# A decoder layer on one core: the order of transfers in SyncE's queue

## The reference

```python
x = layernorm(x + attn(x, w_qkv, b_qkv, w_proj, b_proj))   # causal, 16 heads of 16
x = layernorm(x + slot_attention(x, ctx_1024, ...))        # 3 rounds, GRU cell
x = layernorm(x + mixture_of_experts(x, ...))              # 16 experts, 4 of them kept
# attn
att = einsum('bhqd,bhkd->bhqk', q, k) / sqrt(16); att[not causal] = -inf
y = einsum('bhqk,bhkd->bhqd', softmax(att), v); return y @ w_proj + b_proj
```

## Time and profile before

| what | us |
|---|---|
| median of 3 runs (807.25 to 810.77) | 810.53 |
| the profiled execution | 807.89 |
| its span, first to last instruction | 805.9 |
| attention with its prologue, up to the first context transpose on PE | 239.4 |
| idle time of PE up to 250 us that ended with a DMA of negated maxima | 9.5 |
| idle time of PE up to 250 us that ended with a DMA of operands | 11.8 |

### The profile page before, as it was taken

How to read it: one execution, slowest core, us unless ns; L and a number is a source line. 1 busy time by engine, 2 the same in 40 slices (tenths; PEclk the granted TensorE clock), 3 DMA queues, 4 the chain that set the end, 5 groups by cost and what they waited for, 6 DMA issues and landing times. The chain is left out here.

```text
span 805.9 us, 14338 instructions
## 1 busy us (share of the span) xinstructions
PE 676.9 (84%) x5241; PEld 621.4 (77%) x5256; DVE 478.1 (59%) x1013; ACT 322.1 (40%) x706; POOL 231.3 (29%) x257
## 2 busy tenths in 40 slices
PE   6576989989938899989999799997888657887976
PEld 4454777867727899988989789997888657886976
DVE  3543457647534567676667767676776635546363
ACT  3223435536724345433444344543444224242331
POOL 7112324324421132222230223212243025141432
PEclk9778889989988999989999999999999969989999
DMA  7766255364012000000000000000000000000000
GB/s 239 218 171 202 76 174 155 115 190 105 16 57 101 1 1 1 15 13 0 0 0 26 0 0 0 0 0 1 1 1 2 1 1 1 26 0 26 13 14 27
DMA packets 25676, 40.07 MB, mean 50 GB/s; under 512 B 2336, under 2 KB 11424, under 8 KB 25632
## 3 DMA queue, kind: packets, MB, share of 16 engines
q1 hardware_dynamic: 25632, 39.49, 16.1%
HBM read 24.67 MB, written 14.68 MB: 49 GB/s over the span
## 5 line engine op out<-in xcount | busy, mean ns | idle before, releaser
L1037 DVE TENSOR_REDUCE neg_max<-bank 128x2 f32<-128x512 f32 (+1 forms) x96 | 65.5, 690 | 84.1 <-PE bank L1467 55.2
L1682 PE MATMUL bank<-attn_hl,vg_hl 128*128 128x256 f32 x864 | 111.3, 288 | 1.3 <-ACT attn_hl L673 1.2
L364 PE MATMUL bank<-slots_hl,whhT_hl 128*128 128x256 f32 x864 | 112.4, 289 | 0.0
L364 PEld LDWEIGHTS bank<-slots_hl,whhT_hl 128*128 128x128 f32 x864 | 107.6, 193 | 1.0
L1682 PEld LDWEIGHTS bank<-attn_hl,vg_hl 128*128 128x128 f32 x864 | 106.9, 196 | 1.7 <-ACT attn_hl L673 1.4
L709 ACT ACTIVATE pT<-bank 128x512 f32<-128x512 f32 x96 | 57.0, 597 | 71.6 <-PE bank L1480 55.0
L562 POOL TENSOR_SCALAR_AFFINE_SELECT pT<-pT 128x512 f32<-128x512 f32 x64 | 40.6, 636 | 117.6 <-ACT pT L709 117.5
L624 POOL TENSOR_TENSOR slots_hl<-slots,slots_hl 128x512 fp32r<-128x512 f32 x16 | 20.4, 1275 | 136.9 <-ACT slots_hl L673 136.9
L664 POOL TENSOR_TENSOR hid_hl<-hid,hid_hl 128x512 fp32r<-128x512 f32 x32 | 40.6, 1282 | 61.8 <-ACT hid_hl L673 61.8
L364 PE MATMUL bank<-x2T_hl,keys_hl 128*128 128x256 f32 x384 | 58.0, 309 | 0.0
L364 PEld LDWEIGHTS bank<-x2T_hl,keys_hl 128*128 128x128 f32 x384 | 55.4, 219 | 0.3
(11 more groups left out here) (183 smaller groups left out, 1386.3 us busy)
## 6 DMA issues: line engine op xcount, KB each, us to landing
q_rows<-q_hl SPq DMA_DIRECT2D x24, 256.0 KB
k_rows<-k_hl SPq DMA_DIRECT2D x24, 256.0 KB
q_op<-q_rows SPq DMA_DIRECT2D x32, 192.0 KB, 3.3
k_op<-k_rows SPq DMA_DIRECT2D x16, 384.0 KB, 5.2
xT_in<-in_xT_dram SPq DMA_DIRECT2D x4, 512.0 KB, 4.2
x_in<-in_x_dram SPq DMA_DIRECT2D x8, 256.0 KB, 5.6
c_in<-in_ctx_dram SPq DMA_DIRECT2D x8, 256.0 KB, 2.6
out_dram<-y_out SPq DMA_DIRECT2D x8, 256.0 KB, 2.1
```

What stands on the lines that cost most here:

```text
L364: mm = pe.matmul(dst, left(a), right(b), start=first and n == 0, stop=last and n == 2, skip_group_check=True)
L1037: dve.tensor_reduce(dst, src, AX.X, ALU.max, negate=True).then_inc(max_ok, 1)
L1682: mm = pe.matmul(halves(b)[:, m, :], vg_hl[:, j, v_part, 3 * t + r, q:q + P], attn_hl[:, j, at_part, t, :], start=n == 2 and a + m + t == ...
```

## The change

In the prologue `whhT`, `w_proj` and `eselT` are issued behind the operands of sequence 0, and the second pair's text between its two operand halves; the two x go into the loop. ACT and POOL follow: ACT rounds `v_w_hl` ahead of these three weights and so waits for them later, DVE subtracts them at quad -1. PE makes the values of sequence 1 in the prologue in bank 1. In the loop SP issues operands and `maxima` at each place first, and behind them row writes, x and text.

```diff
@@ SP, prologue
-            sp.dma_start(st_hhT[:, :, :], rows(whhT, NC)).then_inc(w_in[7], 16)
-            sp.dma_start(st_proj[:, :, :], rows(w_proj, NC)).then_inc(w_in[8], 16)
-            sp.dma_start(st_esel[:, :, :], rows(eselT, NC)).then_inc(w_in[8], 16)
             write_q(0, 0)
             write_k(0, 0)
             sp.wait_ge(consts, 15)
             operands(0, 0)
+            load_xT(1)
             operands(0, 1)
+            sp.dma_start(st_hhT[:, :, :], rows(whhT, NC)).then_inc(w_in[7], 16)
+            sp.dma_start(st_proj[:, :, :], rows(w_proj, NC)).then_inc(w_in[8], 16)
+            sp.dma_start(st_esel[:, :, :], rows(eselT, NC)).then_inc(w_in[8], 16)
             write_q(0, 1)
             write_k(0, 1)
-            load_xT(1)
-            load_x(0)
-            load_x(1)
@@ SP, loop (after)
+                if place == 0 and 1 <= 2 * period + 1 < B:
+                    operands(2 * period + 1, 1)
+                elif place == 2 and 2 <= 2 * period + 2 < B:
+                    operands(2 * period + 2, 0)
+                elif place == 4 and 2 <= 2 * period + 2 < B:
+                    operands(2 * period + 2, 1)
+                elif place == 6 and 1 <= 2 * period + 3 < B:
+                    after(sp, consts, 17 if period == -1 else 0)
+                    operands(2 * period + 3, 0)
+                if quad % 2 == 0 and 0 <= quad // 2 + 1 < 2 * B:
+                    maxima(quad // 2 + 1)
                 if place == 0:
-                    if 1 <= 2 * period + 1 < B:
-                        operands(2 * period + 1, 1)
                     if 1 <= period + 1 < PAIRS:
                         write_q(period + 1, 0)
                         write_q(period + 1, 1)
-                    if 2 <= 2 * period < B:
+                    if 0 <= 2 * period < B:
                         load_x(2 * period)
                 elif place == 1 and 1 <= period + 1 < PAIRS:
                     write_k(period + 1, 0)
                     write_k(period + 1, 1)
...
+                elif place == 4 and 1 <= 2 * period + 1 < B:
+                    load_x(2 * period + 1)
+                elif place == 6 and 2 <= period + 3 < PAIRS:
+                    load_xT(period + 3)
-                if quad % 2 == 0 and 0 <= quad // 2 + 1 < 2 * B:
-                    maxima(quad // 2 + 1)
@@ ACT, prologue: v_w_hl first
+            for c in range(NC):
+                for half, blocks in enumerate((slice(0, 4 * P), slice(4 * P, G3))):
+                    act.wait_ge(prep_mm, 2 + 2 * c + half)
+                    act.activation(v_w_hl[:, HI, c, blocks], ...
             act.wait_ge(w_in[7], 16)
             copy(whhT_hl[:, HI, :, :], st_hhT[:, :, :]).then_inc(prep_act, 1)
             act.wait_ge(w_in[8], 32)
             copy(wproj_hl[:, HI, :, :], st_proj[:, :, :]).then_inc(prep_act, 1)
             copy(eselT_hl[:, HI, :, :], st_esel[:, :, :]).then_inc(prep_act, 1)
@@ DVE
+            values_out(1, 1)
...
+                    if (quad, third) == (-1, 0):
+                        dve.wait_ge(prep_act, 10)
+                        step(sub_hi(whhT_hl[:, LO, :, :], st_hhT[:, :, :], whhT_hl[:, HI, :, :]))
+                        dve.wait_ge(prep_act, 12)
+                        step(sub_hi(eselT_hl[:, LO, :, :], st_esel[:, :, :], eselT_hl[:, HI, :, :]))
@@ PE, prologue
             values_of(2, 0)
+            values_of(1, 1)
...
+            pe.wait_ge(v_ok, 2)
```

More of the change, by code:

```diff
@@ L287, in decoder_layer @@
                   (7, 0): [("x1T", 2, -1), ("q", 2, 5)], (7, 1): [("pr", 2, 0)]}
-        BOUNDS = {"neg": (0, 16), "k": (2, 8), "q": (2, 8), "v": (1, 8), "yT": (0, 8), "y": (0, 8), "pr": (0, 8), "x1T": (0, 8)}
+        BOUNDS = {"neg": (0, 16), "k": (2, 8), "q": (2, 8), "v": (2, 8), "yT": (0, 8), "y": (0, 8), "pr": (0, 8), "x1T": (0, 8)}
         QUADS_AND_TAIL = range(-LEAD, QUADS + TAIL)
@@ L567, in inverse_std @@
                 pool.tensor_tensor(std1[:, n % 2, 1, :], std1[:, n % 2, 0, :], half_neg[:, :], ALU.pow).then_inc(rstd1, 1)
-            pool.wait_ge(prep_act, 7)
+            pool.wait_ge(prep_act, 11)
             pool.tensor_tensor(wproj_hl[:, LO, :, :], st_proj[:, :, :], f32(wproj_hl[:, HI, :, :]), ALU.subtract).then_inc(prep_pool, 1)
@@ L741, in _ @@
                 act.activation(qk_w_hl[:, HI, c, :], halves(3)[:, c, :], ACT.Identity, scale=input_col[:, c:c + 1]).then_inc(prep_act, 1)
+            for c in range(NC):
+                for half, blocks in enumerate((slice(0, 4 * P), slice(4 * P, G3))):
+                    act.wait_ge(prep_mm, 2 + 2 * c + half)
+                    act.activation(v_w_hl[:, HI, c, blocks], bank[4 + 2 * c + half][:, 0:blocks.stop - blocks.start],
+                                   ACT.Identity, scale=input_col[:, c:c + 1]).then_inc(prep_act, 1)
             act.wait_ge(w_in[7], 16)
@@ L746, in _ @@
             copy(eselT_hl[:, HI, :, :], st_esel[:, :, :]).then_inc(prep_act, 1)
[L747 to L751, removed]
             for quad in QUADS_AND_TAIL:
@@ L1108, in _ @@
             values_out(0, 2)
[L1109 to L1112, removed]
+            values_out(1, 1)
             for c in range(NC):
                 for half, blocks in enumerate((slice(0, 4 * P), slice(4 * P, G3))):
-                    dve.wait_ge(prep_act, 9 + 2 * c + half)
+                    dve.wait_ge(prep_act, 6 + 2 * c + half)
                     step(dve.scalar_tensor_tensor(v_w_hl[:, LO, c, blocks], bank[4 + 2 * c + half][:, 0:blocks.stop - blocks.start],
@@ L1145, in _ @@
                         variance(2 * period - 1)
-                    elif key == (5, 0) and 1 <= 2 * period + 3 < B:
+                    elif key == (5, 0) and 2 <= 2 * period + 3 < B:
                         values_out(2 * period + 3, BESIDE_BANK["v", 2 * period + 3, 0])
@@ L1574, in _ @@
                     if quad == -LEAD and third == 0:
-                        pe.wait_ge(prep_dve, 15)
-                        pe.wait_ge(v_ok, 1)
+                        pe.wait_ge(prep_dve, 13)
                     if 0 <= quad < QUADS:
```

## The result

The changed kernel takes 821.66 us (820.67 to 821.93, 4 runs); the kernel before took 808.89 in its runs beside it (806.29 to 810.77, 4 runs). The ratio is 1.0158, with a 95% interval of 1.0122 to 1.0194: 12.8 us slower. The prediction had 816, between 808.5 and 821.5: the direction was right, the size about half of what was measured, and the time lies just above the range. On a second chip the same kernel took 822.31 (5 runs, 814.53 to 826.48), ratio 1.0141 (1.0081 to 1.0202). An execution over 1.5% above the fastest of its kernel counts as slow and stays out of the ratios; one of the kernel before took 2191.28 us.

What follows compares the result with a forecast made beforehand. It took SP's queue, with row writes on about half the DMA engines delaying operands, as the limit. Terms -1.9 + 3.05 + 2.6 + 2.6 = +6.4 us on 807.89 gave 814.3, plus 1.6 for the runs' mean: 816, range 808.5 to 821.5.

Steps and rivals of the forecast that it cites:

- What bounds the loop: SP's queue: row writes use about half the DMA engines, 17 us per pair, and the next pair's operands queue behind.
- the edge at natural(16): In pairs 2 and 3 operands arrive under a microsecond before PE needs them; natural(16) starts 0.7 us after landing.
- The place-0 swap: Maxima ahead of query rows: PE's maxima waits go, but rows start 2.85 us later in period 0, 2.6 in period 1.
- Net +1.1 us at the operands: Period 1: of the rows' 2.6 us later start, only 1.1 us reaches the operands' landing (bounds 0 and +2.6).
- The clock: New PE waits for operands at natural(16) and natural(24) are each followed by clock 0.50, costing 2.2 us each.
- Period 0: natural(8), already waiting for operands: +2.85 us for later rows, +0.7 for x, -0.5 given back: +3.05 (bounds +1.5, +3.8).
- The prologue: Moved weights and earlier second text bring natural(4) 1.9 us sooner (bounds -3.4 and +1.5).
- The faster one: Row writes have room, operands land before PE needs them and removed waits are kept: 795 or 797 us; chance 0.06.
- Slower still: Sequence 1's rows land at 49, natural(4) waits until 55 or later, prologue +1.5 or more: 820 to 823; chance 0.15.

Runs made afterwards that it cites:

- experiment 9: The changed kernel run again, unedited, on the chip of the last experiments: 822.31 us (5 runs, 814.53 to 826.48).
- experiment 3: The kernel before with stacked rows reordered so a row write's destination is one dimension of 128 rows, not 8 by 16: 778.93 us, ratio 0.9641.
- experiment 10: The changed kernel, with row writes at place 0 also waiting for the remainders of the next pair's keys: 830.45 us, ratio 1.0258.
- experiment 2: The kernel before with only the maxima at place 0 moved ahead of the next pair's query rows: 822.73 us, ratio 1.0170.
- experiment 5: The changed kernel, with the second operand half of an even sequence issued only when its first half has landed: 817.00 us (10 runs), ratio 1.0097.
- experiment 11: The changed kernel with PE kept busy by extra matmuls during its waits at natural(8), (16) and (24): 814.49 us (10 runs), ratio 1.0068.
- experiment 6: The changed kernel's prologue and x, with the loop's order as in the kernel before: 810.45 us (10 runs), ratio 1.0011.
- experiment 12: The kernel before with reordered rows (destination of 128 rows), plus 13 extra matmuls ahead of the first natural: 780.77 us, ratio 0.9637.
- experiment 1: The changed kernel with the next pair's query rows issued ahead of the maxima again at place 0: 817.73 us, ratio 1.0115.
- experiment 4: The changed kernel with stacked rows reordered so a row write's destination is one dimension of 128 rows: 786.46 us, ratio 0.9720.
- experiment 8: Reordered rows (destination of 128 rows) with the old prologue and the whole new loop order: 779.48 us, ratio 0.9624.
- experiment 7: The prologue as before with the loop's new order, but query rows kept ahead of maxima at place 0: 816.43 us (10 runs), ratio 1.0061.

## Why the prediction was right in direction and half in size

PE's marks against the kernel before, in us; the predicted column adds up the prediction's own terms:

| mark on PE | before | after | moved | predicted |
|---|---|---|---|---|
| natural(4) | 54.93 | 53.80 | -1.1 | -1.9 |
| natural(8) | 80.57 | 81.84 | +1.3 | +1.2 |
| natural(16) | 129.22 | 132.47 | +3.3 | +1.6 |
| natural(24) | 177.48 | 184.52 | +7.0 | +4.2 |
| last heads | 223.73 | 232.82 | +9.1 | +6.4 |
| first context transpose | 239.40 | 250.93 | +11.5 | +6.4 |
| end of the span | 805.9 | 818.7 | +12.8 | +6.4 |

The profile of experiment 9, of the same changed kernel, has natural(8), (16), (24) and the last heads at 83.35, 134.74, 188.81 and 237.14, up to 4.3 us later. So what the table gives in single microseconds holds for one pair of executions.

- **What bounds the loop: right.** The chain from the query rows, written at a DMA share near one half, to the keys, shown by experiments 3 and 10; the edge at natural(16), with 0.7 us to spare, by the new waits.
- **The place-0 swap: right in mechanism,** shown by experiment 2. In period 1 the start came 2.6 us later relative to PE, as said (108.20 less the 1.2 us by which PE was behind at turned(8), against 104.37).
- **The failed step: "Net +1.1 us at the operands".** From query rows to the landing of the keys, 125.60 + 6.8 - 108.20 = 24.2 us, where the earlier trace rows give 24.1: nothing of the 2.6 us was hidden. In period 2 it was half a microsecond (178.00 + 6.5 - 160.49 = 24.0, before 171.11 + 5.6 - 152.17 = 24.5), in experiment 9 nothing (25.2 and 25.1). The queue did hide something: the keys were issued 1.0 and 1.4 us sooner behind the first query row. But they took 1.1 and 0.9 us longer to land, a term that the sum had at nothing. I had asked what the missing wait would make late, and not what it would set free: PE releases the second operand half sooner, and it runs beside the first. In the kernel before, SP issued it when the keys had landed (128.5):

```profile
128.60 0.79 SPq L422 DMA_DIRECT2D q_op<-q_rows  x2
```

  In the changed kernel it is 127.72, ahead of the landing at 132.4. Holding it back gives the 1.0 us back (experiment 5). Against the sum that is 1.6 us in period 1 and 1.2 in period 2, 2.8 of the missing 6.4.
- **The clock: right,** +2.2 predicted, 2.4 by experiment 11, at natural(16) and natural(24).
- **Period 0: right by luck.** natural(8) came at +1.3 for +1.2, but out of -1.1 for -1.9 and +2.4 for +3.05.
- **The prologue: nearly right** (-1.1 for -1.9), and worth nothing that the times of experiment 6 can tell. ACT's wait for the weights and DVE's `whhT` at 50.49 (1.75 us) were where they were put.
- **Not in the sum: 2.4 us between the last heads and the first context transpose.** The same work, at the end of attention, took 15.7 us before and 18.1 after. The projection of the last sequence shows why, first before, then after:

```profile
229.87 1.67 PE L364 MATMUL bank<-wproj_hl,y_hl 128*128 128x256 f32 x12 [1.07 <-DVE y_hl L992]
```

```profile
239.43 2.90 PE L364 MATMUL bank<-wproj_hl,y_hl 128*128 128x256 f32 x12 [0.65 <-DVE y_hl L988]
```

  The clock had already fallen in the second: from 4 to 8 us behind the last heads it is 1.00 before and 0.50 after, though PE's busy time in the 40 us ahead of them agrees to 0.01 us in every ten, all at 1.00. Over the experiments this stretch took 15.8 to 18.0 us with no relation to the edit: 18.0 in experiment 3, and 15.8 in 12, which is the same kernel but for 13 matmuls at its start. So I count it to chance; what decides it is not shown. It may hang on the chip, too: it was 17.6 to 18.0 in experiments 1 to 4, 16.0 to 16.4 in 5 to 8. The last 1.3 us lie in the two later stages, which took 566.5 us before, 567.8 after, and between 566.2 and 571.6 in all the profiles: that is inside the spread. So 3.7 of the missing 6.4 us are in stretches that the change does not touch. In experiment 9, on the other hand, the last heads alone are 13.4 us later than before, and how the loss divides is open.
- **Rivals.** The faster one asked for row writes with room. They have none at a share of one half, but with the reordered rows the room appears, and then the order doesn't matter. "Slower still" named a late second sequence; it wasn't late, the time came from elsewhere.
- **Still open:** why experiments 1 and 7 lose 9 and 7 us by medians, with intervals that start at 1.0059 and 1.0022. The chain told under 7 rests on one profile. The kernel before itself spreads over 20 us, which would fit operands that are due within 0.7 us of their landing, but none of its longer executions was profiled.

## What to carry to other kernels

Before moving a small urgent transfer ahead of a long one, measure the long one's chain to its consumer and the slack at its end: here a wait that was removed upstream of a full queue moved down to the consumer, and brought its slow clock to a place where nothing hid it. A DMA share near one half during a long transfer is a finding in itself; making the destination one dimension of 128 rows gave 30 us, where the largest loss by a reordering of the queue was 14 and none gained. And ask of a removed wait not only what becomes late next, but what is released earlier and will share the queue.

## What the runs showed of the hardware that I had not expected

The same 3.15 MB of row writes, 2 KB per descriptor in both cases, run at 180 GB/s with a destination of 8 by 16 rows side by side and at 335 GB/s with one of 128 rows, each third. The rule of the Trainium skill on how many engines a DMA gets (page "DMA: Bandwidth & Descriptors", section "Why a DMA increments its semaphore by 16 and not by 1") gives 8 and 16, and both traces agree (shares 0.54 and 0.98). A read of 384 KB landed in 5.8 us when the next 768 KB were held until then (experiment 5), and in 6.8 with them issued 2.1 us behind it on the same queue. In all profiles with the old rows, the keys of natural(8), (16) and (24) took 5.4 to 5.8 us where the second half came behind their landing, and 6.0 to 7.9 where it was issued 2.1 to 4.3 us behind them. And a wait of 2.13 us left PE's clock at 1.00 (experiment 7) where one of 2.83 us ended in 0.50. The length of the wait alone doesn't decide it: behind one of 1.90 us in experiment 1 the clock was 0.66 over the next 3.2 us.
